# Attention values in one group per step, and the v projection in two jobs

## The chip, the cores and the metric

The kernel runs on one NeuronCore of a Trainium2 chip. The metric is the device time of one execution in microseconds. TensorE does the matmuls, VectorE (DVE) the row maxima and moments, ScalarE (ACT) the exponentials and the moves out of PSUM, GpSimd (POOL) elementwise work in SBUF, and SyncE (SP) issues the DMAs.

## What is computed

Eight batch rows of 1024 x 256 go through attention with 16 query and 4 key/value heads of 16 (rotary positions on q and k), a layer norm around it, and then a ternary feed-forward layer with a layer norm around it, all in fp32:

```python
x = x + layernorm(attn(layernorm(x), Wq, Wk, Wv, Wo))
x = x + layernorm(ffn(layernorm(x), weight, alpha, bias))
# attn: q, k, v = x@Wq, x@Wk, x@Wv; rope(q), rope(k); k and v repeated for 4 query heads each
#   p = softmax(q @ k.T / sqrt(256)); o = p @ v; return o @ Wo
# ffn:  w = ternary(weight) * alpha; return einsum('bsd,od->bso', x, w) + bias
```

## The kernel before

**Halves and steps.** The work is cut in halves: one batch row `b` and one half `qc` of its 1024 queries. A half has 32 steps (`STEPS`), step `s` being key/value head `s // 8` and key tile `s % 8` of 128 keys. `schedule` (L298) writes the order: a few halves before the loop, the loop over six turns (`Fori`, L316) with two halves each, (b, 1) and (b+1, 0), and the last halves behind it. Every engine runs its own `half` function over the same list, and semaphores join them.

**What a step does.** In each step TensorE (L855 to L878) goes over four pairs. A pair is a matmul of the maxima (L826, scores of the group `LEAD` = 12 steps ahead, written to `smax`) and a matmul of the scores (L870, written to the `ring`). Pairs 0 and 1 fill one side of `smax` (128 x 1024), pairs 2 and 3 the other. Behind pair 1 and behind pair 3 stands one half of the values of step s - 2 (`values`, L832): four matmuls of 128 x 32 weights and 256 columns of the probabilities in fp32, one for each column group of the array, summed in `pv` over eight steps. The last of them raises `pv_step`.

**Who waits.** `smax` has two sides. VectorE reduces each (`reduce_max`, L1030) to one column of `row_max`; a maxima matmul waits until its side has been read (L823). The `ring` has three slots (`RING`) of 512 columns; a score or a job waits until its slot has been read (`ring_free`, L159 and L868). ScalarE reads the scores with an exponential into `probs` (L734), four slots of steps. In step 2 of each eight, ScalarE first copies `pv` into `heads` (L777), and the first values of that step wait for it (L838).

**Jobs.** After its pairs a step may have jobs (`jobs`, L149) which also write a slot of the ring: MT (transposed maxima, each eighth step), and the projections: XT, K, Q and V for the next batch row in half (b+1, 0), Q of its other half in (b, 1), and WO, HT and FF of the half before (`EPI`). V (L913) fills a whole slot: eight tiles of 64 columns, two matmuls each. ScalarE moves every result out (L720, L757 for V); GpSimd copies v into `v_cols` later (`take_v`, L673).

**VectorE's other work.** Moments of the layer norms stand behind the two reduces of a step, by the tables `X_MOM`, `A_MOM`, `Y_MOM` and `F_MOM` (L89): steps 0 to 2 and 5 to 8 (x, in every second half), 9 and 10, 13 to 16, and 28 to 30; in step 20 a cast, in 4 and 22 a reciprocal, and in steps 3, 11, 19 and 27 the split of the maxima.

In the texts below a turn is one pass of the loop; its first half is (b, 1) and its second is (b+1, 0).

Of the kernel before, what the change touches and what calls it, by code (L numbers as in the profile page):

```python
# [38 lines left out]
P = 128  # L39
B, S, D = 8, 1024, 256  # L40
H, HKV = 16, 4
G = H // HKV
HD = D // H
NPAIR = HD // 2
HALF = S // 2
KT = S // P
ST = HALF // P
# [24 lines left out]
LAST = B - 1  # L72
NGROUP = 2 * HKV
FOLD = 2 * G * HALF // P
VCOLS = 2 * HD
# [3 lines left out]
PRO = {11: [("XT", 0, 0), ("XT", 1, 0)], 12: [("XT", 0, 1), ("XT", 1, 1)],  # L79
       13: [("K",)], 17: [("Q", 0, 0)], 18: [("Q", 0, 1)], 20: [("V",)]}  # L80

# [28 lines left out]
class Half:  # L110
# [48 lines left out]
    def ring_free(self, n):  # L159

        if n >= RING:
            return self.base + n - RING + 1
        return self.base - min(((count - n - 1) % RING for count in self.after), default=0)

    def done(self, *job):
# [4 lines left out]
def sandwich_kernel(nc, x, wq, wk, wv, wo, wf, alpha, bias, rope_q, rope_k, out):  # L170
    ctx = ExitStack()
    with ctx:
# [485 lines left out]
        def _(eng):  # L658
# [19 lines left out]
            def half(h):  # L678
                for s in h.steps:
# [8 lines left out]
                    if h.alone and h.pro is not None and s == K_ROT:  # L688
                        eng.wait_ge(ring_read, h.done("V"))
                        for g in range(HKV):  # L690
                            take_v(h, 0, g)
# [14 lines left out]
        def _(eng):  # L706
# [16 lines left out]
            def half(h):  # L723
                n = 0
                for s in h.steps:
# [11 lines left out]
                    for job in h.jobs(s):  # L737
# [19 lines left out]
                        elif kind == "V":  # L757
                            at_least(eng, v_ready, h.pro * HKV)
                            move(v_next[:, :, :].rearrange("p t n -> p (t n)"), src)
                        elif kind == "HT":  # L760
# [21 lines left out]
        def _(eng):  # L782
# [48 lines left out]

            def values(h, s, part):  # L832

                step = h.group0 * KT + s
                g, kt = s // KT % HKV, s % KT
                if part == 0:
                    if kt == 0:
                        at_least(eng, heads_read, h.group0 + s // KT)  # L838
                        if h.qc == 0:
                            eng.wait_ge(v_ready, h.b * HKV + g + 1)  # L840

                    if s >= 0:
                        eng.wait_ge(ring_read, h.done("ST", s, G - 1))
                    else:
                        eng.wait_ge(ring_read, h.base)
                cols = slice(part * HALF // 2, (part + 1) * HALF // 2)
                for j in range(G):
                    mm = eng.matmul(pv[j * VCOLS:(j + 1) * VCOLS, cols], v_cols[:, g, kt, :],  # L848
                                    probs[:, s % PSLOTS, j, cols], start=(kt == 0 and part == 0),
                                    stop=(kt == KT - 1),  # L850
                                    skip_group_check=True)
                if part == 1:
                    mm.then_inc(pv_step, 1)

            def half(h):  # L855
                n = 0
                for s in h.steps:
                    g, kt = s // KT, s % KT
                    mg, mkt = (s + LEAD) // KT, (s + LEAD) % KT
                    for i, j in enumerate(JORDER):  # L860
                        if s < h.maxima:
                            maxima(h, mg, mkt, 1 - i // 2, i % 2)
                        if h.scores:
# [10 lines left out]
                            n += 1  # L874
                        if i % 2 and ((h.scores and s >= LAG) or (h.flush and s < LAG)):
                            values(h, s - LAG, i // 2)
                    for job in h.jobs(s):
# [35 lines left out]
                        elif kind == "V":  # L913
                            for t in range(KT):
                                for dt in range(DT):
                                    mm = eng.matmul(dst[:, t * HKV * HD:(t + 1) * HKV * HD],  # L916
                                                    xT[:, dt, t * P:(t + 1) * P], wv_sb[:, dt, :],
                                                    start=(dt == 0), stop=(dt == DT - 1))
# [226 lines left out]
```

## Time and profile before

| | |
|---|---|
| median of three runs | 1704.89 us (1702.56 to 1709.79) |
| the profiled execution | 1706.93 us, span 1705.0 us |
| TensorE busy | 1494.1 us, 88% |
| VectorE busy | 1389.6 us, 81% |
| ScalarE busy | 1230.1 us, 72% |
| GpSimd busy | 642.6 us, 38% |

The profile is one execution. Times in its rows are microseconds from the start of the span. A matmul's end is modelled, so the distance between starts tells more than the duration. In a row of the timeline, "x8" merges eight records of one kind, and the bracket gives the idle time of the engine before it and what ended that. A matmul in fp32 leaves two records.

### The profile page before, as it was taken

The numbers are of one execution on the slowest core, as the hardware profiler recorded it, in microseconds if no ns is written. First come the engines' busy times: TensorE is split into PE (matmuls) and PEld (weight loads), VectorE is DVE, ScalarE is ACT, GpSimd is POOL, SyncE is SP. The second block draws the span as 40 slices with busy tenths as digits, with TensorE's granted clock in tenths as the row PEclk, the third lists the DMA queues.
The fourth block names the chain that finished last, engine by engine and source line by source line (L and its number), as shares of the span: only waits on it lengthen the run. The fifth ranks groups of instructions, "written<-read, shape, count | busy, mean of one in ns | idle before, by whom it ended". The sixth has DMA issues, their size and how long they took to land.

```text
span 1705.0 us, 41144 instructions
## 1 busy us (share of the span) xinstructions
PE 1494.1 (88%) x13810; PEld 521.7 (31%) x13810; DVE 1389.6 (81%) x1899; ACT 1230.1 (72%) x2357; POOL 642.6 (38%) x703
## 2 busy tenths in 40 slices
PE   4589998989989899998999989998999998889872
PEld 3123233333333233332333323332333322222222
DVE  3697899878998789978898879977899789999914
ACT  1067888767877678777787768776788778878770
POOL 2121442454334443344425544254434354323230
PEclk8579999999999899999999999998999999999996
DMA  2311311113120320213111131202202121111010
GB/s 93 89 42 28 93 37 57 27 41 87 43 63 12 93 58 19 64 29 103 32 49 39 40 87 43 60 14 86 63 22 62 28 77 36 49 33 34 20 42 16
DMA packets 72805, 85.65 MB, mean 50 GB/s; under 512 B 17552, under 2 KB 58384, under 8 KB 71056
## 3 DMA queue, kind: packets, MB, share of 16 engines
q1 hardware_dynamic: 72592, 82.86, 17.3%
q8 instruction: 127, 2.08, 0.5%
q14 instruction: 86, 0.70, 0.1%
HBM read 46.66 MB, written 24.64 MB: 42 GB/s over the span
## 4 chain that ended last, share of the span: by engine, by line
PE 46%; DVE 31%; issue 12%; DMA 4%; POOL 3%; ACT 3%; SPq 1%; DVEq 0%; ACTq 0%; POOLq 0%
DVE row_max L1033 23%; PE pv L848 15%; PE smax L826 14%; PE ring L929 4%; PE ring L910 3%; PE ring L937 3%; PE ring L870 2%; DMA sums<-heads 2%; PE ring L916 2%; ACT heads L777 2%; DMA out<-res 1%; DVE sy_bn L1016 1%; ACT probs L734 1%; POOL res L442 1%; DVE sf_bn L1016 1%
## 5 line engine op out<-in xcount | busy, mean ns | idle before, releaser
L1033 DVE TENSOR_REDUCE row_max<-smax 128x1 f32<-128x1024 f32 x1024 | 1196.5, 1213 | 205.1 <-PE smax L826 203.9
L734 ACT ACTIVATE probs<-ring 128x512 f32<-128x512 f32 x2048 | 1098.8, 597 | 177.8 <-PE ring L870 159.5
L826 PE MATMUL smax<-k_rows,q_rows 48*128 48x512 f16 x2048 | 638.4, 393 | 107.5 <-DVE row_max L1033 89.8
L848 PE MATMUL pv<-probs,v_cols 128*32 128x256 f32 x8192 | 667.1, 398 | 33.4 <-ACT heads L777 33.0
L870 PE MATMUL ring<-q_rows,k_rows 50*128 50x512 f16 x2048 | 637.7, 389 | 0.1
L826 PEld LDWEIGHTS smax<-k_rows,q_rows 48*128 48x128 f16 x2048 | 128.8, 94 | 552.3 <-DVE row_max L1033 399.8
L848 PEld LDWEIGHTS pv<-probs,v_cols 128*32 128x32 f32 x8192 | 163.4, 108 | 429.4 <-issue 305.7
L870 PEld LDWEIGHTS ring<-q_rows,k_rows 50*128 50x128 f16 x2048 | 148.5, 94 | 37.3 <-ACT probs L734 15.7
L453 POOL TENSOR_TENSOR attnT<-pairs,inv_rows 128x512 f32<-128x512 f32 x31 | 39.5, 1273 | 276.0 <-DMA inv_rows<-inv_sums_dram 246.1
L436 POOL TENSOR_TENSOR act<-act,bias_sb 128x256 f32<-128x256 f32 x60 | 42.4, 728 | 118.6 <-ACT act L768 118.6
L721 ACT ACTIVATE rot_in<-ring 128x512 f32<-128x512 f32 x40 | 23.9, 597 | 83.8 <-PE ring L910 71.3
L425 POOL TENSOR_TENSOR actT<-actT,act_parts 128x512 f32<-128x512 f32 x30 | 34.8, 1160 | 107.3 <-DVE act_parts L1082 107.3
L929 PE MATMUL ring<-wo_sb,attnT 128*128 128x256 f32 x256 | 65.5, 401 | 10.5 <-DVE attnT L453 10.5
L343 POOL TENSOR_TENSOR sf_rs<-sf_ve,m_half 128x4 f32<-128x4 f32 x16 | 16.3, 1018 | 132.7 <-DVE sf_ve L1024 132.7
L910 PE MATMUL ring<-xT,wq_sb 128*128 128x512 f32 x128 | 65.0, 632 | 0.0
L721 ACT ACTIVATE act<-ring 128x512 f32<-128x512 f32 x32 | 19.1, 597 | 63.2 <-PE ring L929 63.2
L929 PEld LDWEIGHTS ring<-wo_sb,attnT 128*128 128x128 f32 x256 | 47.5, 195 | 28.9 <-issue 15.9
L343 POOL TENSOR_TENSOR sy_rs<-sy_ve,m_half 128x4 f32<-128x4 f32 x16 | 16.3, 1018 | 101.0 <-DVE sy_ve L1024 101.0
L937 PE MATMUL ring<-wfT,act_parts 128*128 128x256 bf16 x384 | 49.1, 280 | 5.4 <-DVE act_parts L430 5.4
L768 ACT ACTIVATE act<-ring,alpha_sb 128x512 f32<-128x512 f32 x32 | 22.0, 687 | 40.5 <-PE ring L937 40.5
L343 POOL TENSOR_TENSOR sa_rs<-sa_ve,m_half 128x4 f32<-128x4 f32 x16 | 16.2, 1015 | 86.7 <-DVE sa_ve L1024 86.7
L937 PEld LDWEIGHTS ring<-wfT,act_parts 128*128 128x128 bf16 x384 | 35.9, 100 | 22.8 <-issue 10.7
(130 smaller groups left out, 1024.2 us busy)
## 6 DMA issues: line engine op xcount, KB each, us to landing
q_stage_dram<-q_parts SPq DMA_DIRECT2D x48, 256.0 KB, 2.5
q_rows<-q_stage_dram SPq DMA_DIRECT2D x32, 384.0 KB, 5.6
x_in<-in_L_attn_x SPq DMA_DIRECT2D x8, 1024.0 KB, 5.9
pairs<-heads SPq DMA_DIRECT2D x64, 128.0 KB
inv_rows<-inv_sums_dram SPq DMA_DIRECT2D x32, 256.0 KB
res<-in_L_attn_x SPq DMA_DIRECT2D x16, 512.0 KB, 4.5
out<-res SPq DMA_DIRECT2D x16, 512.0 KB, 3.1
k_rows<-k_stage_dram SPq DMA_DIRECT2D x64, 96.0 KB, 3.3
```

Source lines behind the costliest of these rows:

```text
L343: eng.tensor_tensor(rs[:, :], ve[:, :], m_half[:, 0:n], ALU.pow).then_inc(norm, 1)
L436: eng.tensor_tensor(act[:, t, :], act[:, t, :], bias_sb[:, :], ALU.add).then_inc(biased, 1)
L453: eng.tensor_tensor(attnT[:, pair % DT, :], pairs[:, pair % DT, :], inv_rows[:, pair % DT, :], ALU.mult)\
L721: eng.activation(dst, src, ACT.Copy).then_inc(ring_read, 1)
L734: eng.activation(probs[:, s % PSLOTS, j, :], ring[:, n % RING, :], ACT.Exp, scale=score_unit).then_inc(ring_read, 1)
L826: mm = eng.matmul(smax[:, side, c, :], q_rows[at:to, qc, kv * KVP + jp, qt * P:(qt + 1) * P], k_rows[at:to, kv, c * 512:(c + 1) * 512], st ...
L848: mm = eng.matmul(pv[j * VCOLS:(j + 1) * VCOLS, cols], v_cols[:, g, kt, :], probs[:, s % PSLOTS, j, cols], start=(kt == 0 and part == 0), ...
L870: eng.matmul(ring[:, n % RING, :], k_rows[at:to, g, kt * P:(kt + 1) * P], q_rows[at:to, h.qc, g * KVP + j // 2, :], start=True, stop=True)\
L910: mm = eng.matmul(dst, wq_sb[:, dt, a[1], :, :, :].rearrange("p i r h -> p (i r h)"), xT[:, dt, a[0] * HALF:(a[0] + 1) * HALF], start=(dt ...
L929: mm = eng.matmul(dst[:, t * D:(t + 1) * D], attnT[:, dt, (2 * a[0] + t) * P:(2 * a[0] + t + 1) * P], wo_sb[:, dt, :], start=(dt == 0), st ...
L937: mm = eng.matmul(dst[:, t * D:(t + 1) * D], act_parts[:, m, dt, (2 * a[0] + t) * P:(2 * a[0] + t + 1) * P], wfT[:, dt, :], start=(k == 0) ...
L1033: eng.tensor_reduce(row_max[:, g % 2, at:at + 1], smax[:, side, :, :].rearrange("p c n -> p (c n)"), AX.X, ALU.max).then_inc(max_read, 1)
```

## The change

The values of a step become one group of four matmuls over all 512 columns. The group stands behind pair 3, or behind pair 1 in a step which has a job other than MT. The v projection is cut in two jobs of four tiles each, in steps 20 and 21 instead of 20, each with its own slot and its own move. The wait of the first values group (heads read, exponentials of step s - 2, v copied) and the increment of `pv_step` go with the group.

```diff
+ALL = (0, 2)
-       13: [("K",)], 17: [("Q", 0, 0)], 18: [("Q", 0, 1)], 20: [("V",)]}
+       13: [("K",)], 17: [("Q", 0, 0)], 18: [("Q", 0, 1)], 20: [("V", 0)], 21: [("V", 1)]}
...
+    def values_at(self, s):
+
+        if any(job[0] != "MT" for job in self.jobs(s)):
+            return {1: ALL}
+        return {3: ALL}
...
-                        eng.wait_ge(ring_read, h.done("V"))
+                        eng.wait_ge(ring_read, h.done("V", 1))
...
-                            move(v_next[:, :, :].rearrange("p t n -> p (t n)"), src)
+                            move(v_next[:, a[0] * ST:(a[0] + 1) * ST, :].rearrange("p t n -> p (t n)"),
+                                 src[:, 0:ST * HKV * HD])
...
-            def values(h, s, part):
+            def values(h, s, first, last):
...
-                if part == 0:
+                if first == 0:
...
-                cols = slice(part * HALF // 2, (part + 1) * HALF // 2)
+                cols = slice(first * HALF // 2, last * HALF // 2)
...
-                if part == 1:
+                if last == 2:
                     mm.then_inc(pv_step, 1)
...
+                    parts = h.values_at(s) if (h.scores and s >= LAG) or (h.flush and s < LAG) else {}
...
-                        if i % 2 and ((h.scores and s >= LAG) or (h.flush and s < LAG)):
-                            values(h, s - LAG, i // 2)
+                        if i in parts:
+                            values(h, s - LAG, *parts[i])
...
-                            for t in range(KT):
+                            for t in range(ST):
                                 for dt in range(DT):
+                                    at = (a[0] * ST + t) * P
```

## Rows read from the trace of the kernel before

**Rows 1.** The page, part 1: busy us, share of the span, instructions.
```profile
PE 1494.1 (88%) x13810; PEld 521.7 (31%) x13810; DVE 1389.6 (81%) x1899; ACT 1230.1 (72%) x2357; POOL 642.6 (38%) x703
```

**Rows 2.** The chain: start, duration, what; the same job one turn apart.
```profile
701.90 1.92 PE ring L929 x8
...
901.47 1.93 PE ring L929 x8
```

**Rows 3.** The waits of one turn, VectorE: us in total, times, longest.
```profile
DVE row_max L1033 <- PE smax L826: 26.7, 24, 3.0
```

**Rows 4.** Timeline (start, duration, engine, line, what): a Q job and a half step.
```profile
799.43 1.98 PE L910 MATMUL ring<-xT,wq_sb 128*128 128x512 f32 x4
...
801.35 0.39 PE L826 MATMUL smax<-k_rows,q_rows 48*128 48x512 f16 x1
...
801.58 0.38 PE L826 MATMUL smax<-k_rows,q_rows 48*128 48x512 f16 x1
...
801.89 0.64 PE L848 MATMUL pv<-probs,v_cols 128*32 128x256 f32 x8
...
802.46 0.39 PE L826 MATMUL smax<-k_rows,q_rows 48*128 48x512 f16 x1
```

**Rows 5.** Timeline: the V job, and ScalarE and VectorE behind it.
```profile
743.95 3.79 PE L916 MATMUL ring<-wv_sb,xT 128*128 128x64 f32 x32
...
747.67 0.39 PE L826 MATMUL smax<-k_rows,q_rows 48*128 48x512 f16 x1
...
748.30 3.49 DVE L1033 TENSOR_REDUCE row_max<-smax 128x1 f32<-128x1024 f32 x3 [3.00 <-PE smax L826]
748.35 2.06 ACT L734 ACTIVATE probs<-ring 128x512 f32<-128x512 f32 x4
...
750.47 0.39 PE L870 MATMUL ring<-q_rows,k_rows 50*128 50x512 f16 x1
```

**Rows 6.** Timeline: two XT jobs (one row), K, and the reduces beside them.
```profile
716.12 4.71 DVE L1033 TENSOR_REDUCE row_max<-smax 128x1 f32<-128x1024 f32 x4
...
716.74 1.09 PE L891 MATMUL ring<-ident,x_in 128*128 128x128 f32 x8
...
720.05 1.92 PE L903 MATMUL ring<-xT,wk_sb 128*32 128x512 f32 x16
...
721.91 0.39 PE L826 MATMUL smax<-k_rows,q_rows 48*128 48x512 f16 x1
```

**Rows 7.** Timeline: a score and its exponential where ScalarE was idle.
```profile
696.70 0.38 PE L870 MATMUL ring<-q_rows,k_rows 50*128 50x512 f16 x1
...
697.12 0.60 ACT L734 ACTIVATE probs<-ring 128x512 f32<-128x512 f32 x1 [0.37 <-PE ring L870]
```

**Rows 8.** Timeline: step 10, where the values wait for the heads.
```profile
707.92 0.39 PE L826 MATMUL smax<-k_rows,q_rows 48*128 48x512 f16 x1
...
708.99 1.09 ACT L734 ACTIVATE probs<-ring 128x512 f32<-128x512 f32 x2
709.34 0.64 PE L848 MATMUL pv<-probs,v_cols 128*32 128x256 f32 x8 [0.82 <-ACT heads L777]
...
710.55 1.23 DVE L1033 TENSOR_REDUCE row_max<-smax 128x1 f32<-128x1024 f32 x1 [0.77 <-PE smax L826]
...
713.15 2.35 DVE L1033 TENSOR_REDUCE row_max<-smax 128x1 f32<-128x1024 f32 x2
```

**Rows 9.** Timeline: TensorE at the loop's edge.
```profile
782.59 0.60 PE L826 MATMUL smax<-k_rows,q_rows 48*128 48x512 f16 x1 [2.89 <-DVE row_max L1033]
...
784.78 0.60 PE L826 MATMUL smax<-k_rows,q_rows 48*128 48x512 f16 x1
...
786.76 0.60 PE L826 MATMUL smax<-k_rows,q_rows 48*128 48x512 f16 x1
```

**Rows 10.** Granted clock: page, 40 slices in tenths; then a stretch (busy us, clock).
```profile
PEclk8579999999999899999999999998999999999996
...
782.00:789.00 7.00, 6.41 (x40) 1.29 (x40) 3.62 (x3) 3.25 (x6) 3.35 (x3) 0.54 0.38 104
```

## What the change should do to the time

> **What bounds the kernel now.** I read the page's engine shares first [rows 1]: TensorE busy 88%, VectorE 81%, ScalarE 72%. No engine is full, so the waits decide. One turn of the loop (one batch row, two halves, 64 steps) takes 901.47 - 701.90 = 199.57 us [rows 2]; six turns are 1197 of the 1705 us. Inside one turn VectorE waits only for TensorE's maxima: 26.7 us in 24 waits [rows 3]; the rest of its turn is full. So a turn is VectorE's work (about 173 us) plus those 26.7 us, and the change is worth what it does to them. TensorE in turn waits for VectorE in plain steps: the two take turns.
>
> **How a step runs.** With nothing to wait for, TensorE goes pair to pair in 0.23 us (801.35 to 801.58), pair to values in 0.31 (to 801.89), values to the next pair in 0.57 (to 802.46) [rows 4]: 1.11 a half step, 2.22 a step. VectorE's two reduces of a step start 1.14 apart (two merged take 2.35, one alone 1.21 to 1.23 [rows 8]), so a plain step is 2.27 and VectorE-bound, with some moments on top in many steps. A reduce starts 0.63 after the first pair that feeds it (747.67 to 748.30 [rows 5]), and its slot is free again some 1.27 after its own start (1.21 and the signal). That leaves TensorE a lead of 2.27 - 1.27 - 0.63 = 0.37 in which being late costs nothing.
>
> A projection stands between two steps: Q takes 1.92 (799.43 to 801.35) [rows 4], V 3.72 and leaves VectorE idle for 3.00 [rows 5], K 1.86 (720.05 to 721.91) [rows 6].
>
> **What the change does to TensorE.** *Values whole.* Two groups of four 256-column matmuls become one group of four with 512 columns. K is the same form as the new group (128x32, 512 columns, fp32, four column groups), two sets in 1.86 [rows 6]. A line through 0.57 for 256 columns and 1.86 for 1024 gives 0.14 for the way back to a pair and 0.86 for the columns, 1.00 for 512. Bounds: 0.93 (half of K) and 1.14 (two old groups, nothing saved). I take 1.00. A plain step is then 3 x 0.23 + 0.31 + 1.00 = 2.00 of TensorE instead of 2.22, a step with a projection 0.54 + 1.00 + 0.54 = 2.08 instead of 2.22. Over 45 plain and 19 projection steps TensorE is relieved of 12.6 us a turn. Half as many weight loads cost nothing saved: they already lie beside matmuls (TensorE weight loads 31% busy [rows 1]).
>
> *The new stall: the ring.* In a plain step the four scores are now issued behind one another, but the ring has three slots. Score 3 needs the slot of score 0: a score reaches ScalarE's exponential 0.42 after its start (696.70 to 697.12) where ScalarE is idle, the exponential takes 0.60 [rows 7], and a score that waits starts 0.06 behind its end (2.06 from 748.35 is 750.41, score at 750.47) [rows 5]. That is 1.08 from score 0 to score 3, where the bare pairs need 0.69 and the old step 1.34. So a plain step is no shorter than 1.08 + 0.31 + 1.00 = 2.39, over VectorE's 2.27. Where VectorE has moments in the step (0.33 and more each) they cover it. I count 14 plain steps a turn without any; the lead takes most of it, and what is left of these 0.12 is about 0.3 a turn (steps 22 and 23 of the turn's second half).
>
> *Behind a projection* ScalarE first moves the result (0.19 after the next pair, exponential at 0.68 [rows 5]), so score 3 comes at 1.34 and the step takes 1.34 + 1.31 = 2.65. Exposed by 0.4 where no moments follow: once a turn whole (step 7 of the turn's first half), once by a tenth (step 14 of the second).
>
> *Projection steps* hold: pairs 0 and 1, values, pairs 2 and 3, projection. From one to the next it is 2.08 + 1.92 = 4.00 against 4.14; about six such steps a turn give 0.14 each: -0.8.
>
> *Heads.* ScalarE reads the value sums in step 2 of each group of eight, and the values of that step wait for it; in step 10 VectorE is then idle for 0.77 before the second maxima [rows 8]. Step 10 is plain, so values now stand behind pair 3 and the second maxima are fed in time; TensorE is as late as before (ScalarE's exponential at 708.99, slot at 709.65, 1.73 behind pair 0, step end 3.04), but only at the next step, where 1.45 us of moments cover it (710.55 + 1.14 = 711.69, next reduce at 713.15) [rows 8]. This removes 0.77 and in the other half, as I estimate, 0.6: -1.4 a turn. The same step behind FF (step 26) has no such cover: 3.04 - 2.27 = 0.8 idle, about as today, since the same read stands in front of the same pairs. Step 18 has both a wait for the heads and Q: the values there, 1.00 long, push the second maxima by another 0.43: +0.4.
>
> *XT and HT.* Step 12 is hidden today: two XT jobs in some 1.02 (the record says 1.09, with its tail) and no idle in four reduces [rows 6]. Now TensorE enters it late, since VectorE has lost less before it, and two steps of 3.10 against 2.27 leave 0.6 idle; step 19 with HT 0.4: together +1.0.
>
> *V in two jobs.* Each half is 1.86, in steps 20 and 21. Walking the same rules through both steps I get 0.9 + 1.8 idle against 3.0 + 0.2: -0.5. One more ScalarE move costs less than 0.6 on an engine at 72% [rows 1]; GpSimd takes the values a half later, so no reader is near. No DMA moves, and SP's and GpSimd's queues are not passed by anything.
>
> *The loop's edge.* TensorE stands 2.89 behind the branch, and the clock is at its lower level (0.54 granted over 7 us, so mostly 1.2 of 2.4 GHz [rows 10]); the half steps are then 1.98 (784.78 to 786.76) [rows 9]. A whole group there saves about 0.3 a step: -0.3.
>
> **Sum of a turn**: +0.3 + 0.5 - 0.8 - 1.4 + 0.4 + 1.0 - 0.5 - 0.3 = -0.8 us, so -5 us in six turns. Of 12.6 us freed on TensorE nearly all turns into waiting at another place. Outside the loop: the last 12 steps have no maxima and go at TensorE's 2.21; by the ring they take 2.39 (+2), and the three halves around the loop have fewer moments to cover plain steps: +1. Together about -2, on the profiled execution's 1706.9 (span 1705.0): 1705. That execution lies 2.0 over the median, so I forecast **1703 us**.
>
> **Weighed against the Trainium skill.** The rows have the gain per step at 0.14 to 0.22. The Trainium skill (Perfetto Trace Analysis, Optimizing Tensor Performance, Matmuls) says that larger matmuls are more efficient than smaller ones; taken as the whole story it makes this change a gain, which is the first rival below. The trace agrees only in part: 0.14 a step is saved, and the ring takes it.
>
> **Rivals.**
> 1. *The freed time arrives* (faster). If ScalarE's exponentials find the ring free (score 3 at 0.69) and TensorE enters steps 11, 12 and 19 early enough, the losses go (+0.3, +0.5, +0.4, +1.0) and each of the 19 projection steps gives its 0.14 (-2.7): -2.7 - 1.4 - 0.5 - 0.3 = -4.9 a turn, and with 0.22 of the plain step in front of each, another -4.2. Six turns and the outer halves (7.5 turns' worth): -37 to -68. For it: VectorE's waits all stand behind projections. Against: the ring's 1.08 is made of three waits that the rows show [rows 5, 7]. Half of it, about -25, is the likeliest form: 1680.
> 2. *The ring stalls everywhere* (slower). It decides if score 3 comes later than 0.96 and TensorE never has its lead of 0.37, because the group of 1.00 stands in front of pair 0 of each step. Then all 14 uncovered plain steps pay 0.12, the four steps behind projections 0.4, the second maxima of every projection step enters late by 0.2: +1.7 + 1.6 + 3.8, less the 2.7 that I count as gains: +4.4 a turn, +33: 1738. With nothing saved by merging (1.14), 0.14 x 33 steps more. For it: the second maxima can only be fed after the whole group where before a half stood there. Against: moments stand in 30 of the 64 steps. Half of it: 1718.
> 3. *The clock* (slower). TensorE waits in longer pieces between denser bursts. The granted clock is in its top tenth in nearly all slices of the loop, though TensorE waits for VectorE in most plain steps, and it was 0.54 behind the 2.89 us stop [rows 9, 10]. If it fell in one more place a turn for three half steps, VectorE would lose (1.98 - 1.14) x 3 = 2.5 there: 7.5 turns' worth is +19, 1722. The Trainium skill (TensorE: Matmul & The Clock Gate, A second HAM failure mode: psum-queue depth-cycling) describes such a fall from short idles between groups; no row here shows it.
>
> **Chances.** Forecast: 0.42. Rival 1: 0.36. Rival 2: 0.17. Rival 3: 0.05. A measurement of this kernel can tell about 0.5% (8.5 us) from no change. Faster by more than that: 0.37; within: 0.41; slower: 0.22. The range reaches half of rivals 1 and 2: 1674 to 1722. The forecast's own range, from 0.93 and 1.14 for the group (33 steps x 0.07 or 0.14 in part exposed), is 1694 to 1712.
>
> **What would show it.** Right: values groups some 1.00 to the next pair; score 3 at 1.08 behind score 0 in plain steps, waiting for ScalarE; no idle of VectorE at the second maxima of step 10; two V waits of 1 to 1.8 instead of 3.0; a turn of 198 to 200. Wrong: a turn under 196 with VectorE's waits well under 26 us (rival 1), or over 202 with many waits of 0.1 to 0.4 in plain steps (rival 2), or a granted clock that falls in more places of a turn than the edge (rival 3).

## The result, and the profile after

The changed kernel takes **1711.53 us** (median of 20 runs, 1708.5 to 1714.05), the kernel before 1706.95 in the same job (20 runs, 1700.61 to 1711.89): ratio **1.0032**, 95% interval 1.0022 to 1.0042. It is slower by 0.3%, inside the range, but on the other side of no change from the forecast: that had 2 us less than before, and the measured difference is 4.6 us more. (1703 was counted from the median of three runs, 1704.89; from the median of 20 it would be 1705, so 2 us of the distance to 1711.5 are the starting point.) Two executions below, 2586.59 us of whole_proj and 1771.69 us of late_tuned, were slow ones and are in no figure. The profiled execution takes 1712.3 us (span 1710.0), against 1706.9 (1705.0) before.

The page of the kernel after, part 1 (busy us, share of the span, instructions), and from its part 5 the lines of the row maxima, the exponentials, the scores and the values (busy us, mean ns, then idle time before them and its releaser):

```profile
PE 1487.4 (87%) x9714; PEld 455.2 (27%) x9714; DVE 1400.1 (82%) x1899; ACT 1217.0 (71%) x2365; POOL 640.1 (37%) x703
...
L1042 DVE TENSOR_REDUCE row_max<-smax 128x1 f32<-128x1024 f32 x1024 | 1207.0, 1215 | 198.5 <-PE smax L834 195.6
L741 ACT ACTIVATE probs<-ring 128x512 f32<-128x512 f32 x2048 | 1080.6, 603 | 234.9 <-PE ring L878 231.7
...
L878 PE MATMUL ring<-q_rows,k_rows 50*128 50x512 f16 x2048 | 659.6, 391 | 29.6 <-ACT probs L741 22.4
L856 PE MATMUL pv<-probs,v_cols 128*32 128x512 f32 x4096 | 557.8, 617 | 6.3 <-ACT heads L785 6.2
```

TensorE lost 4096 matmuls and only 6.7 us of busy time [rows 1]; its scores now wait 22.4 us for ScalarE to free the ring. VectorE's listed waits for TensorE are 195.6 us, and were 203.9 in the kernel before (its list of waits). By that view alone the kernel should be 8 us faster. The loss is in the other column: VectorE's busy time is 10.5 us more for the same 1899 instructions. The reduces alone account for it, with 1196.5 us before and 1207.0 after.

**Where the time went.** VectorE does 1024 reduces of the row maxima in a fixed order, so the start of the n-th is the same point of the program in every kernel. Between these points the time stands in stretches. Before (first fence) and after (second), stretches from reduce 25 (the half in front of the loop), 89 (six turns), 857 (the three halves behind the loop) and from the last reduce to the end; columns are start:end, length, busy us and instructions of PE, PEld, DVE, ACT, POOL, granted clock, DMA:

```profile
92.79:184.39 91.60, 86.18 (x817) 26.28 (x820) 79.22 (x92) 73.99 (x144) 23.42 (x23) 0.95 0.12 31
184.39:1384.23 1199.84, 1099.97 (x10320) 388.21 (x10320) 1022.18 (x1370) 920.47 (x1765) 503.96 (x549) 0.98 0.19 52
1384.23:1620.45 236.22, 214.43 (x2143) 65.38 (x2142) 213.44 (x275) 193.38 (x373) 76.16 (x86) 1.00 0.14 41
1620.45:1705.00 84.55, 45.09 (x357) 20.01 (x353) 24.11 (x73) 33.09 (x63) 18.46 (x20) 0.79 0.09 29
```

```profile
94.29:190.49 96.20, 89.47 (x574) 22.76 (x573) 81.75 (x92) 73.53 (x145) 23.34 (x23) 0.93 0.13 32
190.49:1385.77 1195.28, 1088.94 (x7248) 334.72 (x7248) 1027.96 (x1368) 910.43 (x1771) 502.57 (x549) 0.98 0.18 51
1385.77:1622.98 237.21, 215.66 (x1471) 56.32 (x1472) 215.69 (x275) 190.70 (x372) 76.03 (x86) 1.00 0.14 40
1622.98:1710.00 87.02, 43.52 (x241) 18.50 (x241) 24.13 (x72) 33.00 (x63) 18.43 (x20) 0.76 0.08 28
```

(The chain of waits alone would mislead: the turn of [rows 2] is 199.57 before and 200.86 after, and single turns differ by 2 us.) Six turns: 1199.8 to 1195.3, **-4.6 us**, as forecast (-5). The half in front of the loop: 91.6 to 96.2, **+4.6**. Behind the loop +1.0, the end +2.4 (forecast +2). The start, where only the v projection is changed, is 1.5 longer; the first reduce stands at 60.7 to 63.6 us in the 14 profiled kernels, without order by what was changed, and I leave it aside.

The lost half, read closer. VectorE's timeline, eight or nine reduces in one piece, before (first fence) and after:

```profile
175.34 10.27 DVE L1033 TENSOR_REDUCE row_max<-smax 128x1 f32<-128x1024 f32 x9
```

```profile
166.64 9.68 DVE L1042 TENSOR_REDUCE row_max<-smax 128x1 f32<-128x1024 f32 x8
...
180.96 10.76 DVE L1042 TENSOR_REDUCE row_max<-smax 128x1 f32<-128x1024 f32 x9
```

Nine reduces take 10.76 us instead of 10.27, and no wait is listed: gaps of 0.1 us are drawn as part of the piece. From reduce to reduce these plain steps take 2.40 to 2.47 us, where before they took 2.26. This is the stall that the forecast worked out from the ring, in a part of that half which has no moments to cover it (its last are in step 8). TensorE in two such steps (after):

```profile
168.41 0.39 PE L834 MATMUL smax<-k_rows,q_rows 48*128 48x512 f16 x1
...
168.90 2.06 ACT L741 ACTIVATE probs<-ring 128x512 f32<-128x512 f32 x4 [0.40 <-PE ring L878]
...
169.22 0.38 PE L834 MATMUL smax<-k_rows,q_rows 48*128 48x512 f16 x1
169.55 0.39 PE L878 MATMUL ring<-q_rows,k_rows 50*128 50x512 f16 x1
169.87 1.06 PE L856 MATMUL pv<-probs,v_cols 128*32 128x512 f32 x8
170.87 0.39 PE L834 MATMUL smax<-k_rows,q_rows 48*128 48x512 f16 x1
```

Pair 0, its score included, at 168.41, the exponential of that score at 168.90, score 3 at 169.55 (1.14 later, and 0.33 behind its own maxima), values 0.32 later, the next pair exactly 1.00 after that: a step of 2.46. The forecast had 1.08 + 0.31 + 1.00 = 2.39.

Not all of the 4.6 us is this stall. Step 27 takes 1.17 us more, and 1.16 of it is two small operations of VectorE on max_parts. GpSimd and VectorE there, before (first fence) and after:

```profile
175.25 0.17 DVE L1053 SCALAR_TENSOR_TENSOR max_parts<-row_max,max_parts 128x16 f16<-128x16 f32 x1
175.26 1.30 POOL L380 TENSOR_TENSOR rot_out<-rot_mul 128x512 f32<-128x512 f32 x1
```

```profile
178.50 1.26 POOL L387 TENSOR_TENSOR rot_out<-rot_mul 128x512 f32<-128x512 f32 x1
178.95 0.85 DVE L1060 TENSOR_SCALAR max_parts<-row_max 128x16 f16<-128x16 f32 x1
...
179.73 1.27 POOL L389 TENSOR_TENSOR rot_out<-rot_mul 128x512 f32<-128x512 f32 x1
179.83 1.20 DVE L1062 SCALAR_TENSOR_TENSOR max_parts<-row_max,max_parts 128x16 f16<-128x16 f32 x1
```

Where GpSimd is in the middle of an operation, VectorE's ends 0.03 us behind it (179.80 and 179.76, 181.03 and 181.00); where VectorE is first by 0.01 us, it takes 0.17. And steps 10 and 11 take 0.71 us more together, at a lower granted clock. The change (first row) and tail_split, described below, which runs the same order of work there (second row):

```profile
121.00:125.00 4.00, 3.67 (x18) 0.59 (x20) 3.61 (x4) 2.17 (x4) 3.77 (x7) 0.57 0.12 39
120.13:124.00 3.87, 3.35 (x28) 0.65 (x28) 3.87 (x4) 2.86 (x6) 3.64 (x7) 1.00 0.13 40
```

In tail_split the two steps are no longer than before. So of the 4.6 us in this profile about 2.7 are steps that the whole group makes longer, 1.2 the meeting with GpSimd and 0.7 the clock.

The waits of one turn, answering [rows 3] (us, times, longest), and VectorE behind the two V jobs, answering [rows 5]:

```profile
DVE row_max L1042 <- PE smax L834: 26.2, 35, 2.6
```

```profile
747.12 1.23 DVE L1042 TENSOR_REDUCE row_max<-smax 128x1 f32<-128x1024 f32 x1 [0.48 <-PE smax L834]
...
749.58 1.23 DVE L1042 TENSOR_REDUCE row_max<-smax 128x1 f32<-128x1024 f32 x1 [0.64 <-PE smax L834]
751.12 1.23 DVE L1042 TENSOR_REDUCE row_max<-smax 128x1 f32<-128x1024 f32 x1 [0.31 <-PE smax L834]
754.13 2.35 DVE L1042 TENSOR_REDUCE row_max<-smax 128x1 f32<-128x1024 f32 x2 [1.79 <-PE smax L834]
```

The one wait of 3.00 us has become four that make 3.22.

### The profile page after: what moved, and what is told of

Its sections match the earlier page's. It is cut to its first block, busy times and chain, and to the rows that moved or that the text cites. A ratio compares the mean times of both kernels' runs of the same rounds, so it can differ in the third digit from the quotient of the medians.

```text
span 1710.0 us, 32979 instructions
## 1 busy us (share of the span) xinstructions
PE 1487.4 (87%) x9714; PEld 455.2 (27%) x9714; DVE 1400.1 (82%) x1899; ACT 1217.0 (71%) x2365; POOL 640.1 (37%) x703
## 3 DMA queue, kind: packets, MB, share of 16 engines
q1 hardware_dynamic: 72592, 82.86, 17.2%
## 4 chain that ended last, share of the span: by engine, by line
PE 46%; DVE 28%; issue 15%; POOL 4%; ACT 4%; DMA 2%; DVEq 0%; SPq 0%; ACTq 0%; POOLq 0%
DVE row_max L1042 22%; PE pv L856 16%; PE smax L834 13%; PE ring L918 4%; PE ring L878 3%; PE ring L938 3%; ACT probs L741 3%; PE ring L946 2%; PE ring L925 2%; PE ring L899 1%; PE ring L931 1%; DVE sf_bn L1025 1%; ACT heads L785 1%; PE ring L911 1%; DVE sy_bn L1025 1%
## 5 line engine op out<-in xcount | busy, mean ns | idle before, releaser
L1042 DVE TENSOR_REDUCE row_max<-smax 128x1 f32<-128x1024 f32 x1024 | 1207.0, 1215 | 198.5 <-PE smax L834 195.6
L741 ACT ACTIVATE probs<-ring 128x512 f32<-128x512 f32 x2048 | 1080.6, 603 | 234.9 <-PE ring L878 231.7
L834 PE MATMUL smax<-k_rows,q_rows 48*128 48x512 f16 x2048 | 625.5, 394 | 111.0 <-DVE row_max L1042 78.2
L878 PE MATMUL ring<-q_rows,k_rows 50*128 50x512 f16 x2048 | 659.6, 391 | 29.6 <-ACT probs L741 22.4
L856 PE MATMUL pv<-probs,v_cols 128*32 128x512 f32 x4096 | 557.8, 617 | 6.3 <-ACT heads L785 6.2
L834 PEld LDWEIGHTS smax<-k_rows,q_rows 48*128 48x128 f16 x2048 | 140.0, 95 | 728.8 <-DVE row_max L1042 565.4
L856 PEld LDWEIGHTS pv<-probs,v_cols 128*32 128x32 f32 x4096 | 81.6, 109 | 161.6 <-issue 106.1
L938 PE MATMUL ring<-wo_sb,attnT 128*128 128x256 f32 x256 | 66.1, 404 | 10.5 <-DVE attnT L460 10.5
L785 ACT ACTIVATE heads<-pv 128x512 f32<-128x512 f32 x64 | 38.0, 593 | 7.1 <-PE pv L856 5.8
```

The costliest lines, as they stand in the source:

```text
L741: eng.activation(probs[:, s % PSLOTS, j, :], ring[:, n % RING, :], ACT.Exp, scale=score_unit).then_inc(ring_read, 1)
L785: eng.activation(heads[:, g % 2, :], pv[:, :], ACT.Copy).then_inc(heads_read, 1)
L834: mm = eng.matmul(smax[:, side, c, :], q_rows[at:to, qc, kv * KVP + jp, qt * P:(qt + 1) * P], k_rows[at:to, kv, c * 512:(c + 1) * 512], st ...
L878: eng.matmul(ring[:, n % RING, :], k_rows[at:to, g, kt * P:(kt + 1) * P], q_rows[at:to, h.qc, g * KVP + j // 2, :], start=True, stop=True)\
L938: mm = eng.matmul(dst[:, t * D:(t + 1) * D], attnT[:, dt, (2 * a[0] + t) * P:(2 * a[0] + t + 1) * P], wo_sb[:, dt, :], start=(dt == 0), st ...
L1042: eng.tensor_reduce(row_max[:, g % 2, at:at + 1], smax[:, side, :, :].rearrange("p c n -> p (c n)"), AX.X, ALU.max).then_inc(max_read, 1)
```

## The experiments

Each kernel is made from the changed one unless it says otherwise. `SPLIT` stands for values in two groups as before, `{1: (0, 1), 3: (1, 2)}`. The stretches of all kernels, in us, each from one profiled execution:

| kernel | half before the loop | six turns | three halves behind | end | ratio to before |
|---|---|---|---|---|---|
| before | 91.6 | 1199.8 | 236.2 | 84.6 | 1 |
| after | 96.2 | 1195.3 | 237.2 | 87.0 | 1.0032 |
| v_split_only | 91.7 | 1197.4 | 236.3 | 83.9 | 0.9996 |
| whole_proj | 91.6 | 1188.3 | 236.7 | 85.1 | 1.0007 |
| whole_plain | 98.4 | 1208.4 | 238.0 | 87.9 | 1.0118 |
| score3_late | 99.8 | 1187.0 | 238.0 | 84.6 | 0.9992 |
| first_split | 92.9 | 1197.6 | 237.2 | 87.3 | 1.0015 |
| tail_split | 97.1 | 1196.7 | 237.2 | 85.0 | 1.0024 |
| values_only | 96.9 | 1194.2 | 237.2 | 87.5 | 1.0030 |
| both_split | 91.2 | 1196.1 | 237.2 | 84.3 | 0.9990 |
| late_loop | 91.4 | 1184.2 | 239.3 | 84.3 | 0.9925 |
| late_tuned | 91.4 | 1183.8 | 233.7 | 83.8 | 0.9914 |
| heads_late | 91.3 | 1181.2 | 237.3 | 85.1 | 0.9908 |
| heads_late2 | 91.1 | 1169.6 | 233.4 | 84.0 | 0.9841 |

### One part at a time: v_split_only, whole_proj, whole_plain, values_only

The v projection in two jobs, values in two groups everywhere:

```diff
     def values_at(self, s):
-        if any(job[0] != "MT" for job in self.jobs(s)):
-            return {1: ALL}
-        return {3: ALL}
+        return SPLIT
```

> The v projection in two jobs, the values in two groups as before. Ring theory (the loss comes from whole values behind pair 3, which drain the ring): this part is harmless, a turn of 199.2 to 199.9 us and 0 to -3 us in all, with two waits of VectorE of about 1.7 us in place of one of 3.0. Rival (the second v job, behind MT in the same step, costs a wait for a ring slot and a second wait of VectorE): a turn of 200.3 or more, +4 us or more.

Measured 0.9996 (0.9986 to 1.0006), as the ring theory had it. The v projection in two jobs is worth nothing that can be measured.

Values whole in the steps with a projection, two groups in the plain ones (`return SPLIT` in place of the second return):

> v in two jobs; the values whole behind pair 1 in steps with a projection, in two groups in all other steps. Ring theory: the good half of the change, without the ring's stall, without the longer way into the loop's edge: each of some 17 projection steps is 0.14 us shorter, a turn of 197 to 198.5, -8 to -18 us against before. Rival (whole groups in projection steps feed the second maxima late and cut VectorE's reduces apart): no gain, 0 to +5 us.

Measured 1.0007 (0.9989 to 1.0025), with runs from 1698.9 to 1715.8 us. The profiled one is at the lower end, so its 1188.3 us for the loop is not the usual run's. The 8 to 18 us that were expected did not come; between the edges a turn is 0.6 us shorter.

The reverse, whole behind pair 3 in plain steps alone (`return SPLIT` in place of the first):

> v in two jobs; the values whole behind pair 3 in steps without a projection, in two groups in steps with one. Ring theory: the bad half: plain steps of 2.39 instead of 2.27 where no moments cover them, 2.65 behind a projection, and the loop's edge later by 0.4 us or more: a turn of 200.5 to 203, +5 to +18 us. Rival (the loss sits in the projection steps): a turn under 199.6 and a time no longer than before.

Measured 1.0118 (1.01 to 1.0136): the plain placement alone costs 20 us. That is a little over the expected 5 to 18. By its profile 6.8 us are the half in front of the loop, 3.3 the end, 8.6 the loop, of which 7 at its edges. Of the 6.8, 2.9 are steps 29 and 30 of that half, where the granted clock was 0.50 from 185 to 189 us.

Values whole as in the change, the v projection in one job:

> The changed kernel with the v projection in one job again, so the placement of values alone. If the two parts add: v split alone came to 0.9996, the change to 1.0032, so this one comes to 1.0036 (1.0025 to 1.0045), with the step of the v projection in the first half back to about 7.7 us for its two steps (8.4 with the change). Rival, the parts collide: whole values behind pair 1 of step 20 and 21 and the half jobs take the ring from each other, and with one job the whole is better than that sum, at or under 1.002. The forecast's own term for the v halves was -0.5 us a turn, which would give 1.0050.

Measured 1.0030 (1.0016 to 1.0043), as the change itself. So the placement of the values makes the loss; what the two V jobs add is not to be told from nothing.

### Where the loss is: first_split, tail_split, both_split

```diff
     def values_at(self, s):
+        if self.very_first:      # first_split; tail_split: if s >= self.maxima; both_split: either
+            return SPLIT
```

> The changed kernel with one thing put back: in the half step in front of the loop (first query half of the first batch, 32 steps that have scores but no moments of a finished tile on VectorE) values go in two groups again, behind the second and the fourth pair. Theory of the exposed step: in that half VectorE has nothing but the reduces, so each whole group costs it (uncovered plain steps 2.46 us against 2.27 before, heads steps +1.1 us), and this half is 4.6 us longer with the change while the six turns are 4.6 us shorter. Then the half comes back to 91.6 to 92.1 us, the turns stay 4 to 5 us below before, and the whole is 4 to 5 us under the changed kernel: ratio to before 0.9985 to 1.000. Rival, the loss is in the whole kernel and the profile of one run misplaces it (clock): the ratio stays at 1.002 to 1.004.

> The changed kernel with one thing put back: in the last 12 steps that have scores but no row maxima, values go in two groups again. Theory of the exposed step, as the forecast costed it: without maxima between the scores, a whole group of 1.00 us after score 3 leaves VectorE uncovered by about 0.2 us a step, so about 2 us come back: the stretch from reduce 1 of the last half to the end gets back from 87.0 to about 84.8 us, ratio to before 1.002. Rival, the 2.4 us at the end come from the heads, the output transposes or the epilogue and not from the values' place: under 0.7 us come back, ratio 1.003.

> The changed kernel with both put back: values in two groups in the half in front of the loop and in the last 12 steps without maxima, whole everywhere else. Theory: these two places cost 4.4 and 2 to 2.4 us, what lies between gains 4.6 us in the six turns and gives 1 back behind them, so the sum is 3 to 5 us under before: ratio 0.9975 to 0.9990. Rival, the profile's sum by stretches does not hold for the median of many runs (the run with the first half alone put back came to 1.0015 where 1.0006 was expected): 1.000 to 1.0015.

Measured: 1.0015 (0.9999 to 1.003), 1.0024 (1.0012 to 1.0036) and, with both, **0.9990** (0.9976 to 1.0003). The stretches answer one by one: the first half goes from 96.2 to 92.9 and, with both, 91.2 us; the end from 87.0 to 85.0 and 84.3. first_split missed its expected 0.9985 to 1.000: its one profile kept 1.3 us there, with the granted clock at 0.91 in that half (0.95 before); 1.0 is in step 3 and 0.7 in steps 10 and 11, all at the lower clock, less 0.4 at step 27. both_split has the same placement in that half and none of this. Together the two places are 0.42% of 1707, 7.2 us; the stretches show 7.7. What is left is the forecast's gain in the loop, and it is too small to tell from nothing.

### The late score: score3_late, late_loop

In plain steps the whole group stands between the maxima and the score of pair 3, so that the score's wait for its ring slot is spent on values:

```diff
+                    late = h.scores and h.values_at(s) == {3: ALL}
 ...
+                        if late and i == 3 and 3 in parts:
+                            values(h, s - LAG, *parts[3])
                         if h.scores:
 ...
-                        if i in parts:
+                        if i in parts and not (late and i == 3):
```

> The changed kernel, but in plain steps the whole group stands between the maxima and the score of pair 3, so that score 3 comes 1 us later and its ring slot is long free. Ring theory: no wait of 0.2 to 0.6 us of that score for ScalarE, plain steps of TensorE near 2.2 instead of 2.40, 2 to 8 us faster than the changed kernel. Rival (the loss sits at the loop's edge and in a lower granted clock in front of it): as slow as the changed kernel, within 2 us, +3 to +7 us against before.

Measured 0.9992 (0.9978 to 1.0007): 12.9 us less than before in the six turns, 8.2 us more in front of them. Of the 8.2, 4.5 are steps 29 and 30 behind a stop of TensorE of 1.61 us, with the granted clock at 0.50 from 184 to 191 us. The same kernel, with two groups in the half in front of the loop and in the last steps without maxima:

> Values whole as in the changed kernel, with the whole group of a plain step between the row maxima and the score of pair 3 (as in the run with score 3 late), but in two groups in the half step in front of the loop and in the last 12 steps without maxima. Theory: the late score 3 gains 12.9 us in the six turns, where VectorE's moments cover the step, and loses 8.2 us in front of the loop, where nothing does; taking that half out leaves 12 us under before less what the end costs: ratio 0.992 to 0.995. Rival, the 12.9 us is the clock of one run (151.5 against 156.9 us of low clock explains at most 2.5 us of it) and the rest is spread: ratio 0.997 to 0.9995.

Measured **0.9925** (0.9908 to 0.9942), as that theory had it. What it gains on the changed kernel is for the most part in the heads step behind FF and the step after it. TensorE and ScalarE in step 26 of a turn's first half, after (first fence) and with the late score in the form of heads_late2, where this step is the same (second):

```profile
665.50 0.39 PE L834 MATMUL smax<-k_rows,q_rows 48*128 48x512 f16 x1
...
666.66 2.06 ACT L741 ACTIVATE probs<-ring 128x512 f32<-128x512 f32 x4
667.32 0.39 PE L878 MATMUL ring<-q_rows,k_rows 50*128 50x512 f16 x1 [0.58 <-ACT probs L741]
667.63 1.06 PE L856 MATMUL pv<-probs,v_cols 128*32 128x512 f32 x8
668.63 0.39 PE L834 MATMUL smax<-k_rows,q_rows 48*128 48x512 f16 x1
...
669.27 1.22 DVE L1042 TENSOR_REDUCE row_max<-smax 128x1 f32<-128x1024 f32 x1 [0.78 <-PE smax L834]
```

```profile
651.62 0.39 PE L838 MATMUL smax<-k_rows,q_rows 48*128 48x512 f16 x1
...
652.79 3.16 ACT L745 ACTIVATE probs<-ring 128x512 f32<-128x512 f32 x6
652.95 1.06 PE L860 MATMUL pv<-probs,v_cols 128*32 128x512 f32 x8
653.95 0.39 PE L885 MATMUL ring<-q_rows,k_rows 50*128 50x512 f16 x2
654.18 0.59 PE L838 MATMUL smax<-k_rows,q_rows 48*128 48x512 f16 x2
...
654.81 1.22 DVE L1049 TENSOR_REDUCE row_max<-smax 128x1 f32<-128x1024 f32 x1 [0.19 <-PE smax L838]
```

ScalarE copies FF's result and the heads first, so the exponential of score 0 starts 1.16 us after pair 0. In the changed kernel score 3 waits for it and the values for score 3: next pair 3.13 behind pair 0, VectorE idle 0.78. With the values first, score 3 comes at 653.95 without a wait and the next pair at 654.18, 2.56 behind pair 0, and 0.19 is idle. That is the 0.8 which the forecast left "about as today", taken back.

### Each placement where it pays: late_tuned, heads_late, heads_late2

Read from the intervals between reduces (medians of six turns), steps 5 and 13 are longer with the change (3.65 to 4.00, 4.15 to 4.64) and step 17 with the late score (2.44 to 2.79): steps 5 and 17 are projection steps behind a plain one and step 13 stands behind the short XT jobs. The reading is that the whole group pushes the second maxima there, where nothing was late before; whole_proj, where only the projection steps are whole, has the same 0.35 and 0.45 at steps 5 and 13. Steps 6, 9, 25 behind another projection are 0.15 shorter each. late_tuned therefore puts SPLIT into steps 5, 13, 17 and into a few uncovered plain steps (18; 0, 1, 2, 6, 7 in the two last halves), on top of late_loop.

> The kernel with the late score 3 in the loop (0.9925), with values in two groups also in the first projection step of a group of them (steps 5, 13, 17), in step 18 where it is plain, and, in the two halves behind the loop that have no projections of their own, in steps 0, 1, 2, 6 and 7. Theory: a whole group behind pair 1 pushes the second maxima of a step whose predecessor was plain by 0.35 to 0.5 us (the intervals of steps 5, 13 and 17 grew by 0.35, 0.50 and 0.35), and only the steps behind another projection gain their 0.15; so 1.2 us a turn come back, step 18 and 19 give 0.3, and 2 us behind the loop: 9 to 11 us under the late score 3, ratio 0.986 to 0.988. Rival, the time only moves on: the next projection step, now entered after two groups, gives back its 0.15 and the lead that was won, and the ratio stays at 0.991 to 0.993.

Measured 0.9914 (0.9892 to 0.9936), not the 0.986 to 0.988 of the theory but its rival's 0.991 to 0.993. Steps 5 and 13 came back to 3.71 and 4.22, as meant, step 17 did not (2.96), and the three halves behind the loop gave 5.6 us (the granted clock over them was 0.99 in late_loop and 1.00 in late_tuned). The loop gave 0.4: between the edges a turn is 179.7 us instead of 180.4, at the edge 17.6 instead of 17.0. heads_late asks what the plain steps contribute:

```diff
-        return {3: ALL}
+        if s % KT == LAG:
+            return {3: ALL}
+        return SPLIT
```

> As the run before it, but values whole (with the late score 3) only in the plain steps that wait for the heads (the third of each eight), and in the projection steps that stand behind another; two groups in every other plain step. Theory: plain steps gain nothing from the whole group, whose time VectorE covers, and the gain of the late score 3 sits in the heads steps (10 in each half -0.7 and -0.9, 26 in each -0.5 us, and what follows it): then this is equal to the run before within 3 us, ratio 0.986 to 0.989. Rival, TensorE's 0.22 us saved in each plain step gives it the lead with which it enters the projections: without it 0.15 to 0.4 us come back in front of each of the nine projection groups of a turn, 8 to 15 us in all: ratio 0.991 to 0.995.

Measured 0.9908 (0.989 to 0.9927), the same within the interval and short of the expected 0.986 to 0.989. So outside the heads steps the whole group of a plain step is worth nothing here, or less, since this kernel also has a loss of its own: steps 18 and 19 of the first half took 3.6 us each, against 2.3 and 3.0. The trace of heads_late there, TensorE's rows, then two stretches with the clock in the third column from the right:

```profile
432.41 0.39 PE L838 MATMUL smax<-k_rows,q_rows 48*128 48x512 f16 x1 [1.27 <-DVE row_max L1049]
...
434.30 1.94 PE L860 MATMUL pv<-probs,v_cols 128*32 128x512 f32 x8
```

```profile
432.00:434.00 2.00, 1.15 (x7) 0.46 (x7) 2.00 (x3) 1.09 (x2) 1.79 (x4) 0.95 0.18 66
434.00:438.00 4.00, 4.00 (x23) 0.64 (x21) 2.23 (x3) 1.79 (x4) 0.94 (x3) 0.60 0.03 6
```

TensorE stood 1.27 us, two microseconds later the granted clock is 0.60, mostly at 1.2 of 2.4 GHz, and one group takes 1.94 instead of 1.06. It is so in five of the six turns; in the first the clock stays at 1.00 and the two steps take 0.5 us more instead of 2. heads_late2 puts step 18 (and 2 and 18 of the last halves) back to two groups.

> The kernel with the whole group in heads steps alone (0.9908), with step 18 of the halves that have no Q there, and steps 2 and 18 of the two last halves, in two groups again. In that kernel the value sums of step 17 end late, ScalarE reads the heads at 431.36 in front of the exponentials, TensorE stands 1.27 us and then the granted clock is 0.60 over 434 to 438 us: steps 18 and 19 of the turn's first half take 1.9 us more than before. Theory: that place alone is 1.9 us a turn and 2 us more behind the loop; without it the loop is 28 to 30 us under before and the ratio 0.983 to 0.986. Rival, TensorE's clock falls at another step instead (the loop edge, as in the kernel before it, took 1 us more where step 18 took 2 less): ratio 0.988 to 0.991.

Measured **0.9841** (0.9815 to 0.9866), as the theory had it, 1677.22 us: 27 us faster than the kernel before by the ratio and 29 by the two medians. The clock no longer falls at that place, but the stop is still there, as it is in every turn of the kernel before (1.25 to 1.27):

```profile
434.22 0.39 PE L838 MATMUL smax<-k_rows,q_rows 48*128 48x512 f16 x1 [1.27 <-DVE row_max L1049]
```

```profile
434.00:438.00 4.00, 3.78 (x36) 1.19 (x36) 4.00 (x5) 3.19 (x6) 2.53 (x6) 1.00 0.11 39
```

So the stop alone does not bring the clock down. What differs is the work around it, the whole group in step 18. A long stretch of a turn (from step 2 of its first half to step 29 of its second), then the edge of the loop (five steps), in three kernels: before, after, heads_late2.

```profile
590.79:773.47 182.68, 168.75 (x1611) 61.44 (x1611) 157.38 (x210) 142.87 (x275) 75.91 (x84) 1.00 0.17 45
773.47:790.38 16.91, 13.25 (x111) 3.44 (x109) 12.94 (x19) 10.15 (x20) 8.71 (x8) 0.80 0.40 121
```

```profile
594.56:776.57 182.01, 166.94 (x1131) 52.53 (x1131) 158.54 (x211) 141.57 (x277) 75.67 (x84) 1.00 0.17 46
776.57:794.82 18.25, 14.82 (x81) 3.62 (x80) 12.94 (x19) 10.00 (x20) 8.68 (x8) 0.72 0.40 128
```

```profile
581.92:760.58 178.66, 167.62 (x1435) 58.89 (x1435) 157.47 (x212) 142.46 (x277) 74.73 (x84) 1.00 0.18 48
760.58:776.64 16.06, 12.34 (x111) 3.38 (x109) 12.84 (x19) 10.17 (x20) 9.69 (x9) 0.89 0.34 104
```

Over the six turns the first stretch is 182.8 on average before (182.5 to 183.4), 182.2 after (182.0 to 182.6), 179.1 in heads_late2; at the edge 17.2, 17.0 and 15.9, with single edges from 12.8 to 19.2 us. Nearly all the noise of a turn sits at the edge, where the clock falls; between the edges it is 1.00, and 0.3 us can be read.

## Why the prediction was right, and where it failed

The forecast had the change 2 us faster, and it is 4.6 us slower.

- **The size of a group**: 1.00 forecast, 1.00 measured (169.87 to 170.87). Right.
- **The ring stall**: right as a mechanism, 1.14 from score 0 to score 3 instead of 1.08, since the exponential starts 0.49 behind the score in these steps and not 0.42 [rows 7]; a step exposed to it takes 2.46 (less in some).
- **A turn**: -0.8 forecast, -0.76 measured, -0.64 of it between the edges. That the sum agrees so well is in part luck, since its terms missed by more. Step 7 behind a projection +0.29 (forecast +0.4), the heads steps 10 -0.68 and -0.87 (-1.4 together; -1.55). XT: step 12 of the second half +0.66 (0.6), but K in step 13 +0.50, and Q in step 5 of the first half +0.35, which had no term; step 19 +0.2 (0.4). The step with heads and Q, 18 of the second half, -0.1 (+0.4). Steps behind another projection -0.15 at 6, 9 and 25, as forecast, and -0.41 at step 9 of the second half. V: -1.86, +2.27 and -0.28 in its three intervals, +0.1 (forecast -0.5): four waits of 0.48, 0.64, 0.31 and 1.79 instead of one of 3.00; a half job takes 1.93 to the next pair, not 1.86, and the second one waits 0.32 for the ring behind the job in front of it. The edge's -0.3 came as -0.16, within its noise.
- **The step that failed** is the half sentence "the three halves around the loop have fewer moments to cover plain steps: +1". The four halves outside the loop were summed by analogy with a turn, and the term should have been +5.6. Three of them do cost +1.0. The half in front of the loop costs **+4.6**: it has the moments of x up to step 8 and no others, since no tile is finished yet, and behind step 8 every exposed step pays. Ten such steps are 0.08 to 0.32 longer (2.1 us), V 0.5, K 0.5, less 0.3 at step 3 and 0.1 at step 18: 2.7 us. Ten steps at 2.39 - 2.27, both in the prediction, are 1.2 us, so part of it could have been worked out from its own numbers, had this half been walked through. Each such step was mis-sized as well: most are 0.20 longer (2.26 to 2.46), not 0.12, and K and V had no cost. Its 0.8 for a heads step without cover did not come: step 26 is 0.29 longer, and step 10 at the full clock (tail_split) 0.05. The rest stands in no term: 1.2 us at step 27, where VectorE meets GpSimd's operation, and 0.7 at steps 10 and 11 by the clock, which in tail_split and values_only did not fall there but in step 29.
- **The last 12 steps**: +2 forecast, +1.5 measured. From the last reduce to the last exponential it is 31.4 us before and 33.0 after, and 31.4 again in tail_split. The other 0.9 of the end's 2.4 lies behind the last exponential. Right in size.
- **The range's ends.** Rival 1 (the freed time arrives) did not happen with this placement. Time of its order did come in heads_late2, where score 3 no longer stands in front of the values in the heads steps and groups are merged only where that pays: the loop is 30 us shorter, 22 between the edges and 8 at the edges. Rival 2 (the stall everywhere) was right for the uncovered part of one half. Its test, a turn over 202 us, failed, so it looked refuted in the loop while it decided the result outside. (Half of its +33 on 1705 is 1721, not 1718; nothing hangs on it.) Rival 3 (the clock) is small but not nothing: the granted clock is 1.00 between the edges and 0.93 against 0.95 in the half in front, 0.7 us there. All five kernels with whole groups in the plain steps of that half show such a fall in their one profile, worth 0.7 to 4.5 us; of the nine others only first_split does. heads_late shows one at the same place in five turns of six; at its steps 18 and 19 these take 1.6 us more than the turn without it. The Trainium skill (TensorE: Matmul & The Clock Gate, A second HAM failure mode: psum-queue depth-cycling) puts such falls down to short idles between groups; here the short idles of each plain step left the clock at 1.00, and single stops of 1.25 to 1.7 us had a fall behind them in some kernels and none in others.
- **What stays open.** What brings the clock down is not shown. The length of the stop is not enough: 1.27 us in heads_late has a fall behind it and 1.27 us in heads_late2 and before has none; in the half in front, 1.25 us at step 10 has one in the changed kernel and none in tail_split, and the 1.68 us of the kernel before has none. Nor was it tried alone whether GpSimd's rotations can be moved off VectorE's small operations: that the two meet is read from the traces, in all five kernels whose plain steps are exposed in that half (step 27 takes 4.39 to 4.67 us) and in none of the nine others (2.85 to 3.32).

## What to carry to other kernels

Sum a change separately for each stretch that has different cover, the short ones around the loop as well: here six turns gave 4.6 us and a single half took them back, 2.7 of it in steps that stand without cover there. A merge of matmul groups saves TensorE time (0.14 us a step), but what it does to the order in which a small ring is filled and freed is worth more in either sign: the merged group was 1.2% slower behind score 3 in all plain steps and, in front of score 3 and only where ScalarE is late, part of a kernel 1.6% faster. And compare kernels at the same instruction of the bottleneck engine, not by its listed waits, in which 256 short stalls looked better than 181 long ones.

## What the runs showed of the hardware

- Gaps of about 0.1 us between VectorE's reduces are in no list of waits. Reduces that follow without a gap start 1.13 apart though one alone takes 1.22, so breaking a row of them costs 0.09 each, and it is booked as busy time: 1196.5 us of reduces before and 1207.0 after, for the same 1024.
- A small operation of VectorE in SBUF (128x16) takes 0.17 us alone. Started while an elementwise operation of GpSimd was running, it took up to 1.2 and ended 0.02 to 0.04 us behind that: so in all 31 of the 128 on max_parts that took over 0.3 us in the changed kernel.
- A stop of TensorE of 1.25 to 1.7 us is no sure sign of a lower clock: in the kernel before it stood 1.25 to 1.27 us in step 18 of each turn's first half, and the granted clock stayed at 1.00.
- The time between the last reduce of the loop's body and the next turn is no fixed number: the five steps at the edge took 13.7 to 19.2 us in the six turns of the kernel before, at a granted clock of 0.64 to 0.80. whole_plain lost 7 us there over six turns and whole_proj gained 8, while a turn between the edges differed from before by +0.2 and -0.6 us. What in a placement sets the edge was not settled.
